# A chunked gated delta rule on one core: merged leaves written by VectorE into the compact array, and the next chunk's decay products row by row on GpSimd

## The reference, cut to what matters

```
q, k, v = silu(causal_conv4(x @ W)) ...      # each (T, H, D)
a = sigmoid(x @ Wa + ba)                     # a decay per token, head and channel
beta = sigmoid(x @ Wb + bb)
for t in range(T):                           # per head, S is 128 x 128
    y = S @ (k_t * D**-0.5)
    S = a_t[..., None] * S - (b_t * (y - v_t))[..., None] * (k_t * D**-0.5)[None, :]
    o_t = S @ q_t
x = x + (layernorm(o) * sigmoid(x @ Wg)) @ Wo
x = x + mixture_of_experts(layernorm(x))     # top 2 of 8, and a shared expert
```

## Time and profile before

| | |
|---|---|
| median of 3 runs | 3173.81 us (3172.24 to 3183.9) |
| profiled execution | 3174.62 us, its span 3172.8 us |
| TensorE granted clock, mean | 0.977 of full speed |
| PE / DVE / ACT / POOL busy over the span | 89% / 73% / 51% / 42% |

### The profile page before, as it was taken

The page is one execution under the profiler, slowest core; times in us unless marked ns, Lnnn a source line. Parts: engine busy times, 40 slices in busy tenths (PEclk is TensorE's granted clock), DMA queues, the critical chain, the costliest instruction groups (busy, mean ns, idle before and its releaser), DMA issues. The chain is left out here.

```text
span 3172.8 us, 48588 instructions
## 1 busy us (share of the span) xinstructions
PE 2838.1 (89%) x14144; PEld 2012.0 (63%) x14144; DVE 2322.8 (73%) x4837; ACT 1605.5 (51%) x3516; POOL 1317.6 (42%) x1574
## 2 busy tenths in 40 slices
PE   7999999678898898988989898898888989869999
PEld 3555555366676776666766676776767767645555
DVE  6777777578888778887787878788887788724332
ACT  6666666445555555554554555555555555421111
POOL 3666767624443444443443434444334444310000
PEclk9999999889999999999999999999999999979999
DMA  3655565631222322222323222322223222034220
GB/s 133 242 202 231 234 241 202 225 60 34 54 42 41 60 51 54 43 41 42 69 41 55 41 42 43 67 46 51 42 41 65 46 54 42 8 105 89 55 44 14
DMA packets 449884, 261.23 MB, mean 82 GB/s; under 512 B 402672, under 2 KB 414672, under 8 KB 447472
## 3 DMA queue, kind: packets, MB, share of 16 engines
q1 hardware_dynamic: 449664, 258.51, 31.5%
HBM read 153.42 MB, written 105.05 MB: 81 GB/s over the span
## 5 line engine op out<-in xcount | busy, mean ns | idle before, releaser
L265 DVE SCALAR_TENSOR_TENSOR A_acc<-A_psY,A_w,A_acc 128x410 f32<-128x410 f32 (+1 forms) x720 | 419.2, 637 | 151.6 <-ACT A_acc L334 151.6
L1155 ACT ACTIVATE B_WL<-B_psT 64x128 f32<-64x128 f32 (+3 forms) x480 | 148.6, 310 | 512.4 <-PE B_psT L1576 512.4
L840 POOL TENSOR_TENSOR B_WT<-B_WT,B_G 128x128 f32<-128x128 f32 (+2 forms) x224 | 183.0, 817 | 513.0 <-PE B_psT L1576 493.3
L405 PE MATMUL A_psY<-A_xT,A_w 128*128 128x413 f32 (+1 forms) x960 | 347.2, 510 | 9.1 <-PE A_psAG L411 7.7
L192 POOL TENSOR_TENSOR A_outs<-A_outs,A_acc 128x410 f32<-128x410 f32 (+1 forms) x240 | 229.7, 987 | 215.5 <-ACT A_outs L342 215.5
L1068 DVE TENSOR_TENSOR B_NC<-B_NC,B_psM 128x256 f32<-128x256 f32 x480 | 199.1, 415 | 143.9 <-PE B_psM L1603 101.8
L405 PEld LDWEIGHTS A_psY<-A_xT,A_w 128*128 128x128 f32 x960 | 180.2, 189 | 165.5 <-issue 164.2
L822 POOL TENSOR_TENSOR B_PQ<-B_PQ,B_G 128x256 f32<-128x256 f32 x128 | 125.8, 983 | 368.3 <-DVE B_WT L1036 368.3
L1071 DVE TENSOR_REDUCE B_W<-B_NC 128x64 f32<-128x320 f32 x512 | 248.7, 486 | 17.6
L1603 PE MATMUL B_psM<-B_BD,B_WL 128*128 128x128 f32 x1536 | 237.6, 296 | 12.6
L334 ACT ACTIVATE A_acc<-A_psY,A_w 128x410 f32<-128x410 f32 (+1 forms) x240 | 166.2, 692 | 162.9 <-PE A_psY L405 161.2
(11 more groups left out here) (197 smaller groups left out, 6703.5 us busy)
## 6 DMA issues: line engine op xcount, KB each, us to landing
B_KQ<-scr SPq DMA_DIRECT2D x96, 512.0 KB, 6.8
scr<-A_outs SPq DMA_DIRECT2D x48, 615.0 KB, 3.5
scr<-A_outag SPq DMA_DIRECT2D x32, 615.0 KB, 5.2
scr<-A_outs SPq DMA_DIRECT2D x48, 409.0 KB, 2.5
A_xc<-nbeta SPq DMA_DIRECT2D x16, 1024.0 KB, 5.9
B_A<-scr SPq DMA_DIRECT2D x32, 512.0 KB, 5.0
B_C<-scr SPq DMA_DIRECT2D x32, 512.0 KB, 5.9
B_G<-scr SPq DMA_DIRECT2D x32, 512.0 KB, 4.6
```

Of the source, the lines that this page charges most:

```text
L265: nc.vector.scalar_tensor_tensor(a, y, w[:, s, col:col + 1], a, ALU.mult, ALU.add)\
L405: last = nc.tensor.matmul(psY[p][:, y0:y0 + HALO + t1 - t0], wp[:, p, kt, :], xT[:, kt, t0:t1 + HALO], start=kt == 0, stop=kt == KT - 1)
L840: tt(dst, dst, gr, ALU.mult).then_inc(wsc.sem, 1)
L1155: copy = lambda out, in_: nc.scalar.activation(out, in_, ACT.Copy)
```

## The change

Two things change. First, for the last leaf of the merges of four and eight leaves (j = 3, 7, 11), L1073 writes straight into its place in `WC`. ScalarE's second copy is turned round: it now copies that leaf from `WC` back to `WT[:, j]`, and stands behind the `WL` copy. TensorE waits for the first copy alone (and for L1073), and `scale_left` on GpSimd, which scales `WT[:, j]` with the others, waits for the copy back. Second, `decays` leaves VectorE, but for the first chunk. GpSimd makes the six rows one by one (`row_decays`, 256 elements in each partition), placed as `rows(0)` to `rows(5)` in its loop; `dec` counts six to a chunk.

```diff
-DEC = 3
+DEC = 6
...
+            def row_decays(g, *parts):
+                a, e = by_leaf_row(A[:, g % 2]), E[:, g % 2]
+                products = ((RR_, a[:, 1], a[:, 2]), (B_, e[:, RR_], a[:, 3]), (F_ + 1, a[:, 0], a[:, 1]),
+                            (B_ + 1, a[:, 2], a[:, 3]), (F_ + 2, e[:, F_ + 1], a[:, 2]), (F_ + 3, e[:, F_ + 2], a[:, 3]))
+                for k in parts:
+                    row, x, y = products[k]
+                    if k == 0:
+                        loaded(pool, "A", g)
+                        wait(pool, nc0, 2 * g - 3, 5)
+                    else:
+                        wait(pool, dec, g, {1: 1, 4: 3, 5: 5}.get(k, 0))
+                    tt(e[:, row], x, y, ALU.mult).then_inc(dec.sem, 1)
...
                 wait(pool, tps, g, j + 1)
+                if p >= 2:
+                    wait(pool, wc, g, {3: 2, 7: 4, 11: 6}[j])
...
                 past(g, 2)
                 gates(0, 1)
+                rows(0)
                 past(g, 3)
                 queries(2)
                 scale_left(g, 3)
                 gates(2)
                 past(g, 4)
                 scale_right(g, 5)
                 gates(3)
+                rows(1)
                 past(g, 5)
                 queries(3)
                 scale_left(g, 5)
                 scale_right(g, 7, (0,))
                 past(g, 6)
                 scale_right(g, 7, (1,))
+                rows(2)
                 past(g, 7)
                 scale_left(g, 7)
+                rows(3)
                 past(g, 8)
                 scale_right(g, 9)
+                rows(4)
                 past(g, 9)
                 scale_left(g, 9)
+                rows(5)
                 scale_right(g, 11)
...
-            def decays(g, parts=(0, 1)):
...
-                    tt(e[:, F_ + 1:B_ + 2:3], a[:, 0:3], a[:, 1:4], ALU.mult).then_inc(dec.sem, 1)
...
-                    tt(e[:, F_ + 2:B_ + 1:4], e[:, F_ + 1:RR_ + 1:3], a[:, 2:4], ALU.mult).then_inc(dec.sem, 1)
...
-                    tt(e[:, F_ + 3], e[:, F_ + 2], a[:, 3], ALU.mult).then_inc(dec.sem, 1)
+            def first_decays():
...
-                    tt(WT[:, j] if j % 2 else WR[:], W[:, :, lf], E[...], ALU.mult).then_inc(wt.sem, 1)
+                    p, n, _ = merge_of(j)
+                    if j < JM and p >= 2:
+                        to = WC[:, 0:H * n].rearrange("p (h t) -> p h t", h=H)[:, :, n - R:n]
+                    else:
+                        to = WT[:, j] if j % 2 else WR[:]
+                    tt(to, W[:, :, lf], E[...], ALU.mult).then_inc(wt.sem, 1)
...
-                    elif j == 8 and more:
-                        decays(g + 1, (0,))
                     elif j == 9:
                         if more:
-                            decays(g + 1, (1,))
                             mask_own(g + 1, 0, 0)
...
-                        if p >= 2:
-                            wait(act, wt, g, j + 1)
-                            left_compact(g, j, (j,))
                         wait(act, tps, g, j + 1)
                         wait(act, mps, g, 2 * j)
...
                         copy(WL[0:rows_, 0:w_], psT[0:rows_, 0:w_]).then_inc(wl.sem, 1)
+                        if p >= 2:
+                            wait(act, wt, g, j + 1)
+                            copy(WT[:, j], WC[...][:, :, n - R:n]).then_inc(wc.sem, 1)
...
-                            wait(pe, wc, g, {3: 2, 7: 4, 11: 6}[j])
+                            wait(pe, wc, g, {3: 1, 7: 3, 11: 5}[j])
```

More of the change, by code:

```diff
@@ L578, in recurrence @@
         kl, kc = Count(sem("leaf_keys"), 2), Count(sem("block_keys"), 3)
-        wc = Count(sem("left_compact"), 6)
+        wc = Count(sem("left_rearranged"), 6)
         wec = Count(sem("w_end"), 2)
@@ L852, in _ @@
                 queries(1)
+                rows = lambda *parts: row_decays(g + 1, *parts) if g + 1 < NCH else None
                 past(g, 2)
                 gates(0, 1)
+                rows(0)
                 past(g, 3)
@@ L904, in _ @@
             wait(dve, zeros, 0, NZERO)
-            def decays(g, parts=(0, 1)):
[L908 to L915, removed]
-                    tt(e[:, F_ + 1:B_ + 2:3], a[:, 0:3], a[:, 1:4], ALU.mult).then_inc(dec.sem, 1)
-                if 1 in parts:
-                    wait(dve, dec, g, 1)
-                    tt(e[:, F_ + 2:B_ + 1:4], e[:, F_ + 1:RR_ + 1:3], a[:, 2:4], ALU.mult).then_inc(dec.sem, 1)
-                    wait(dve, dec, g, 2)
-                    tt(e[:, F_ + 3], e[:, F_ + 2], a[:, 3], ALU.mult).then_inc(dec.sem, 1)
+            def first_decays():
+                loaded(dve, "A", 0)
+                wait(dve, dcp, 0, 2)
+                a, e = by_leaf_row(A[:, 0]), E[:, 0]
+                tt(e[:, F_ + 1:B_ + 2:3], a[:, 0:3], a[:, 1:4], ALU.mult).then_inc(dec.sem, 3)
+                wait(dve, dec, 0, 3)
+                tt(e[:, F_ + 2:B_ + 1:4], e[:, F_ + 1:RR_ + 1:3], a[:, 2:4], ALU.mult).then_inc(dec.sem, 2)
+                wait(dve, dec, 0, 5)
+                tt(e[:, F_ + 3], e[:, F_ + 2], a[:, 3], ALU.mult).then_inc(dec.sem, 1)
             def coefs(h):
@@ L1072, in chunk @@
                     wait(dve, ws, g, j + 1)
-                    tt(WT[:, j] if j % 2 else WR[:], W[:, :, lf], E[:, g % 2, B_:B_ + R, :, j].rearrange("p r h -> p h r"), ALU.mult).then_inc(wt.sem, 1)
+                    p, n, _ = merge_of(j)
[3 more added lines that the diff above has]
+                        to = WT[:, j] if j % 2 else WR[:]
+                    tt(to, W[:, :, lf], E[:, g % 2, B_:B_ + R, :, j].rearrange("p r h -> p h r"), ALU.mult).then_inc(wt.sem, 1)
                     if j % 2 == 0:
@@ L1134, in chunk @@
                     add_state(g, i)
-            decays(0)
+            first_decays()
             nc.vector.memset(NC[:, 1], 0.0).then_inc(zeros.sem, 1)
@@ L1350, in chunk @@
                         copy(WL[0:rows_, 0:w_], psT[0:rows_, 0:w_]).then_inc(wl.sem, 1)
+                        if p >= 2:
+                            wait(act, wt, g, j + 1)
+                            copy(WT[:, j], WC[:, 0:H * n].rearrange("p (h t) -> p h t", h=H)[:, :, n - R:n]).then_inc(wc.sem, 1)
                     if j == 13:
```

## The result

The changed kernel takes 3140.28 us (median of 6 runs, 3137.19 to 3156.69) against 3175.55 before: a ratio of 0.9894 (95% interval 0.987 to 0.9918), 35 us less. A second measurement on another chip gave 0.9882 (0.9862 to 0.9903). The time lies at the low end of the range, 3139 to 3198; but the likeliest case was no change, 3169, and that was not what came. The profiled execution took 3142.96.

A forecast was written before the change was run, and what follows sets the result against it. No engine is full; the chain of leaves bounds the kernel, VectorE at some leaves. Leaf terms sum to -0.17 us in 31 chunks (5.3 us), plus 0.4 in the last: 3169 us from 3174.62, range 3139 to 3198.

The forecast's parts named there:

- the likeliest case: Whole kernel: -0.17 us a chunk, 3169 us, no measurable change; chance 0.45, of its own between 3155 and 3184.
- a chunk that is shorter by over a microsecond: Sign named beforehand, for one chunk of the recurrence: if seen, the forecast would be wrong.
- rival (b): Leaves 6 and 7: meetings are cheap; a row at 0.71 gives -1.01 us a chunk, 3143 us; chance 0.14.
- Price of a GpSimd row product: GpSimd's six rows: 1.13 us each for three with two strided factors (0.71 to 1.57), 0.86 for the others.
- the two meetings: After leaves 6 and 7, VectorE steps wait for GpSimd's third and fourth product: +0.83 us each (0 to +1.13).
- Leaf 3: Transposes start earlier without ScalarE's copy of the last leaf, until TensorE's other matmuls end: -0.14 us (-0.35 to +0.4).
- Leaves 8 and 9: Decays leave VectorE there, TensorE is late next: -1.75 us, not the -3.4 of the three instructions.
- Leaf 10: Sixth product pushes scale_right(11) over L1073 and the sums' scaling, which wait: +0.33 us together (0 to +1.3).
- Leaf 11: Direct write takes a copy out of the chain, then VectorE is the bound again: -0.27 us (0 to -0.33).
- Rival (a): Leaf 7: scale_left comes too late for its step, one meeting as today; -0.85 us a chunk, 3148 us; chance 0.2.
- Rival (c): First, third and fourth product dearer through strides: at 1.5 us each, +0.94 us a chunk, 3203 us; chance 0.21.

The follow-up runs named there:

- the filler: Identity transposes that nothing reads, put into TensorE's pauses: changed kernel 0.9798; kernel before, after leaves 9 and 10 1.0016, at all four pauses 0.9934.
- the kernel with the late scaling: Changed kernel with third and fourth product behind leaf 8's scaling, filler transposes, and GpSimd's scaling for leaf 11 after leaf 10's own work: 0.9733, 3093.32 us.

## Why the prediction was right and wrong

*The range held, by 1.3 us; the order of events was the forecast's, its prices were not, and luck had a part.* The likeliest case was too high by 29 us, and by the prediction's own sign, a chunk that is shorter by over a microsecond, it was wrong: the chunk is shorter by 1.41. What came is rival (b), the cheap meetings, which had a chance of 0.14. The 44 us of the leaves alone would have led from 3173.81 to about 3130, below the range; that the time lies inside it is due to the clock, which took some 10 us back and which no case had. (The sum also started from the profiled execution and not from the median, 0.8 us too high.)

The step that failed is "Price of a GpSimd row product ... I take 1.13", and with it the two meetings at +0.83: of the 1.24 us between -0.17 and -1.41 the meetings make 0.86. The product without interference takes 0.66: here the first one in the changed kernel, which ends as the leaf's L1095 begins and does not delay it. The last line is leaf 3's transposes in the kernel before.

```profile
1309.80 0.66 POOL L787 TENSOR_TENSOR B_E<-B_A 128x256 f32<-128x256 f32 x1
...
1310.42 0.27 DVE L1095 TENSOR_TENSOR B_WE<-B_W,B_E 128x64 f32<-128x64 f32 x1
...
1310.66 0.35 ACT L1174 ACTIVATE B_WE<-B_WT 128x192 f32<-128x192 f32 x1
...
1311.11 0.41 PE L1594 MATMUL B_psT<-ident,B_WE 128*128 128x128 f32 x2
...
1324.88 0.41 PE L1576 MATMUL B_psT<-ident,B_WE 128*128 128x128 f32 x2
```

The lower end that the prediction gave, 0.71, was nearer than the row it chose; at that price rival (b) has meetings of 0.41 and came to 3143. A meeting costs what is left of the product when VectorE's step could begin; taking 0.83 over from two meetings with products of twice the elements was the error behind it. The run with one product of 512 elements shows the dependence. As an estimate from the rows, the wait is the end of GpSimd's record less the start of VectorE's, less 0.13: that gives 0.82 and 0.83 for the two meetings in the earlier trace rows, 0.42, 0.90 and 0.36 for the third product, `scale_left` and the fourth product in the changed kernel, and 0.89 for the one product of 512 elements. VectorE's steps were longer by 0.83, 0.83, 0.41, 0.90, 0.36 and 0.87.

In the Trainium skill, "SBUF — State Buffer", section "Who interferes with whom", the later instruction waits for the whole of the other. The trace agrees in kind: the steps that waited have two operands in SBUF, and moving the products beside PSUM readers freed them. What the step waits for is what is left of the other: 0.41 of a product of 0.66, of which the rest ran before the record of VectorE's step before had ended.

*Leaf 3* (-0.25 for -0.14): the leaf's own product (L1073, now L1095) did not have to wait for a product of 0.66, and TensorE takes the transposes up 0.10 after ScalarE's first copy ends, at 1311.01, as it did 0.11 after the second one before (1324.77 and 1324.88). So the whole 0.24 of the second copy came off; TensorE's other matmuls, which the forecast took for the next bound, did not hold the transposes back. *Leaves 8 and 9* (-1.82 for -1.75): TensorE was the next bound, as said, so of the 3.4 us that VectorE gave up no more than about half came off the chain. *Leaf 10* (+0.17 for +0.33): right in kind, as the kernel with the late scaling shows. *Leaf 11* (-0.31 for -0.27): right.

*Rival (a)* did not come: `scale_left` kept 0.13 of its lead. *Rival (c)* did not either: stride did not make the products dearer. *What no case had* is the clock: 16 us lost before and 26 after, by the two profiles. Before leaf 14's half-clock stretch in chunk 14 TensorE paused 0.86 and 0.39 us, and for 1.08 us within it:

```profile
1614.79 0.30 PE L1594 MATMUL B_psT<-ident,B_WR 128*64 128x128 f32 x1 [0.86 <-DVE B_WR L1095]
1615.47 0.46 PE L1604 MATMUL B_psM<-B_PQ,ident 128*128 128x128 f32 x2 [0.39 <-DVE B_PQ L1048]
...
1617.51 1.06 PE L1518 MATMUL B_ring<-ident,B_KQ 128*128 128x128 f32 x4
...
1619.65 1.73 PE L1635 MATMUL B_psM<-ident,B_WE 128*128 128x128 f32 x7 [1.08 <-ACT B_WE L1174]
```

Chunk 10 has the same pauses (0.87, 0.38 and 1.08) and no fall; why one chunk falls and another does not stays open. That the falls hang on these pauses is shown by the filler, in both kernels: it took away those at the places where it stood. No run has the same transposes where TensorE does not pause, so whether the added work alone would do it is not shown. The table of leaves by itself would have been misleading without that: the change took 44 us out and the clock kept about 10 of them.

## What to carry to other kernels

In these runs a product that moved from VectorE to GpSimd cost nothing beside VectorE instructions that read PSUM, and what was left of its length beside those that read SBUF twice; so place it by VectorE's operands, not by GpSimd's free time. Splitting it gained little (0.73 for two meetings, 0.83 for one of twice the length). Price a moved instruction by rows with the same operands, and where none exists, give the lower bound as much weight as the nearest one. Once the leaves are shorter, look at the granted clock window by window: here half-clock stretches cost as much as the meetings (26 and 23 us), and transposes that nothing reads, put into TensorE's pauses of about a microsecond, gave that back.

## What the runs showed of the hardware that was not expected

A GpSimd product of 256 elements whose two factors lie in the same array with a step of four takes 0.66 us (back to back two in 1.29), less than one with one such factor and one dense one, 0.87; the denser gates took 0.71, and two factors from two arrays in steps of eight 1.13. Why is open. The 13 transposes of the identity cost no time that the leaves show (leaf 14 to the next chunk 14.16 us with and without them), and the clock at its full level gave 1.2 to 5.4 us back for each stretch. Filling the pauses after leaves 9 and 10 alone moved the falls to later ones (ratio 1.0016), filling all four places was worth 0.9934.
